# A four-layer graph network on one core: a third sort of the edges, the edge records fetched in the dense stages, and node degrees summed in layer 1

## The reference

```python
edge_index = jnp.stack([src, dst])
xn = _layernorm(x, axis=-1)
x = x + _L0_gnn_ref(xn, ..., src, dst) + _L0_mix_ref(xn[None], ...)[0]
x = x + _L0_ffn_ref(_layernorm(x, axis=-1)[None], ...)[0]
...
# layer 0, edges
e = jax.nn.leaky_relu(el[src] + er[dst], NEG_SLOPE)
score = e @ attn
smax = jax.ops.segment_max(score, dst, num_segments=N)
ex = jnp.exp(score - smax[dst])
ssum = jax.ops.segment_sum(ex, dst, num_segments=N)
out = jax.ops.segment_sum(el[src] * (ex / ssum[dst])[:, None], dst, num_segments=N)
```

## Time and profile before

| what | us |
|---|---|
| median of three runs | 9504.5 (9498.88 to 9510.58) |
| the profiled execution on the device | 9501.75 |
| its span in the profile | 9499.6 |
| sort by target, with keys, chunk order and parts | 262.6 |
| all stages of the order by source | 398.6 |
| opening of layer 0 | 716.1 |
| attention of layer 0 | 1341.0 |
| the nine dense stages from `close0` to `open2` | 1035.7 |
| sum pass of layer 1 | 1113.5 |

### The profile page before, as it was taken

One profiled execution on the slowest core, in us unless ns is written; L12 is line 12 of the kernel. 1 busy time (PEld: TensorE's weight loads), 2 busy tenths in 40 slices (PEclk: granted clock), 3 DMA queues, 4 the chain that ended last, 5 costly groups with the idle time before them and its releaser, 6 DMA issues. The chain is left out here.

```text
span 9499.6 us, 92227 instructions
## 1 busy us (share of the span) xinstructions
PE 6037.2 (64%) x26290; PEld 4579.3 (48%) x26290; DVE 4854.0 (51%) x13537; ACT 2032.6 (21%) x5038; POOL 4347.3 (46%) x4412
## 2 busy tenths in 40 slices
PE   0012306999996875555755555553883788886699
PEld 0001105788874443333544433342872677775466
DVE  7773406888884532222343222275114588887433
ACT  0001003555542210000120000022221233333322
POOL 0476775666650047777004777702001577772000
PEclk9998657999997887777777777775996777777799
DMA  0001003333330133333102333301871233331000
GB/s 14 6 2 36 10 2 94 89 90 90 90 80 9 54 114 105 105 105 105 24 12 75 105 105 105 105 7 24 301 272 41 78 97 99 97 98 45 12 14 21
DMA packets 404417, 697.22 MB, mean 73 GB/s; under 512 B 154143, under 2 KB 267784, under 8 KB 403421
## 3 DMA queue, kind: packets, MB, share of 16 engines
q0 software_dynamic: 206848, 480.68, 18.8%
q1 hardware_dynamic: 197076, 210.68, 7.0%
HBM read 631.46 MB, written 59.47 MB: 73 GB/s over the span
## 5 line engine op out<-in xcount | busy, mean ns | idle before, releaser
L641 PE MATMUL sum_sum<-sum_rows,sum_hot 128*125 128x256 f32 x3520 | 1268.3, 524 | 956.4 <-DMA sum_rows<-el_table,dst_order_row 465.9
L658 POOL DMA_INDIRECT att_rows<-el_table,dst_order_row x1520 | 1476.3, 971 | 755.8 <-issue 377.5
L641 PEld LDWEIGHTS sum_sum<-sum_rows,sum_hot 128*125 128x125 f32 x3520 | 868.5, 258 | 1356.2 <-issue 1029.2
L602 POOL DMA_INDIRECT sum_rows<-rel_table,src_order_row x880 | 836.9, 951 | 888.2 <-ACTq L593 620.4
L602 POOL DMA_INDIRECT sum_rows<-el_table,dst_order_row x880 | 835.3, 949 | 806.0 <-ACTq L593 538.3
L554 POOL DMA_INDIRECT dst_order_record<-records,dst_order_row x784 | 835.1, 1065 | 582.0 <-PEq L458 297.3
L624 DVE TENSOR_TENSOR gnn_acc<-gnn_acc,sum_sum 125x256 f32 x440 | 181.4, 412 | 1591.1 <-PE sum_sum L641 1585.7
L800 PE MATMUL att_found<-gnn_to_dst,att_hot_t 125*128 x1760 | 442.5, 395 | 40.9 <-issue 40.3
L824 PE MATMUL att_sum<-att_rows,att_hot 128*125 128x261 f32 x1760 | 443.7, 394 | 0.0
L1140 PE MATMUL att_sum<-att_rows,att_hot 128*125 128x265 f32 x1280 | 421.2, 485 | 2.5 <-DVE att_rows L1031 2.4
L658 POOL DMA_INDIRECT dst_order_record<-el_table,dst_order_row x240 | 240.9, 1004 | 333.8 <-SPq L962 239.2
(11 more groups left out here) (775 smaller groups left out, 12136.3 us busy)
## 6 DMA issues: line engine op xcount, KB each, us to landing
block_w<-in_L_ffn_W_dram SPq DMA_DIRECT2D x112, 512.0 KB, 6.2
block_w<-in_L_ffn_W_dram SPq DMA_DIRECT2D x56, 1024.0 KB
att_rows<-el_table,dst_order_row POOLq DMA_INDIRECT x1520
rel_table<-open_st SPq DMA_DIRECT2D x25, 784.0 KB
sum_rows<-rel_table,src_order_row POOLq DMA_INDIRECT x880, 2.7
sum_rows<-el_table,dst_order_row POOLq DMA_INDIRECT x880, 2.7
dst_order_record<-records,dst_order_row POOLq DMA_INDIRECT x784, 2.3
pairs<-zeros SPq DMA_DIRECT2D x1, 7168.0 KB
```

Of the source, the lines that this page charges most:

```text
L602: nc.gpsimd.indirect_dma_start(rows[l][:, g, :], None, table, bass.IndirectOffsetOnAxis(ap=o["row"][:, k:k + 1], axis=0)).then_inc(s[f"row ...
L641: last = nc.tensor.matmul(slot(u), hot[u % HOTS_S][:, g, :], rows[l][:, g, :], start=(g == 0), stop=(g == G - 1))
L658: nc.gpsimd.indirect_dma_start(rows[l][:, g, 0:width], None, table, bass.IndirectOffsetOnAxis(ap=o["row"][:, k:k + 1], axis=0)).then_inc(s ...
```

## The change

`order_by_pair` sorts the edges by target and source: the low bits of the key are the source, so `row` is the source at once and nothing has to be fetched for layer 0. `order_by_edge` sorts by target and edge number a third time, after the order by source, and keeps the edge numbers in `edge`; it has no unit tiles. `fetch_records` gathers by `edge`, and no longer in the sorts or in `open0`, but in nine dense stages up to `open2`, after which `unpack_records` stands. Records have three words. `build_attend0` loses the three columns (L860 and L761 go) and the degree phase goes. Layer 1's `build_sums` makes the degrees: it loads target, weight and attribute of all edges, and for 200 of the 220 units VectorE makes one-hot marks of the node in its tile and of the tile, the latter also times weight and attribute, and TensorE multiplies them into one PSUM bank. In that pass there are seven row buffers instead of ten; in both passes 12 marks and 12 PSUM slots, and `BEHIND` is 8.

```diff
-HOTS_S = 14
-SLOTS_S = 16
-BEHIND = 10
+HOTS_S = 12
+SLOTS_S = 12
+BEHIND = 8
+DEGS_S = 2
-REC = 4
+REC = 3
-SHARES = (14, 190, 30, 6, 8, 18, 14)
-EARLY = sum(SHARES)
+SHARES = {"close0": 78, "open0g": 66, "ffn0s": 42, "ffn0e": 100, "open1": 156, "close1": 25, "open1g": 37, "ffn1e": 146, "open2": 134}
...
+def order_by_pair(nc, c, I, o):
...
+                own(v.tensor_scalar(dst_i[:], dst_i[:], 12, 0x20000000, ALU.logical_shift_left, ALU.bitwise_or))
+                own(v.tensor_tensor(edges, dst_i[:], src_i[:], ALU.bitwise_or))
...
+                own(v.tensor_scalar(o["row"][:, main], bits, 0xFFF, None, ALU.bitwise_and))
+        build_unit_tiles(nc, c, "dst_tiles", o)
+def order_by_edge(nc, c, I, o):
...
+                own(nc.vector.tensor_scalar(o["edge"][:, 0:CHUNKS_S], key_c[:].bitcast(I32), 0x1FFFF, None, ALU.bitwise_and))
...
-        nc.gpsimd.indirect_dma_start(o["record"][:, k, :], None, o["records"], bass.IndirectOffsetOnAxis(ap=o["row"][:, k:k + 1], axis=0)
+        nc.gpsimd.indirect_dma_start(o["record"][:, k, :], None, o["records"], bass.IndirectOffsetOnAxis(ap=o["edge"][:, k:k + 1], axis=0)
...
+                def make_ends(n, own):
+                    l, part, here = n % DEGS_S, slice(n * G, n * G + G), slice(n % DEG_UNITS * G, n % DEG_UNITS * G + G)
+                    if n % DEG_UNITS == 0:
+                        part_edges(n, own)
+                    if n >= DEGS_S:
+                        dve.wait_ge(s["degree_summed"], n - DEGS_S + 1)
+                    v.tensor_tensor(end[l][:], row_of(iota_p[:, 0:R], G), col_of(in_tile[:, here], R), ALU.is_equal)
+                    own(v.tensor_tensor(terms[l][:, :, 2, :], row_of(iota_p[:, 0:TILES], G), col_of(of_tile[:, here], TILES), ALU.is_equal))
+                    v.tensor_tensor(terms[l][:, :, 0, :], terms[l][:, :, 2, :], col_of(of_edge["weight"][:, part], TILES), ALU.mult)
+                    v.tensor_tensor(terms[l][:, :, 1, :], terms[l][:, :, 2, :], col_of(of_edge["attr"][:, part], TILES), ALU.mult).then_inc(s["ends_ready"], 1)
...
+                    if u < N_D:
+                        pe.wait_ge(s["ends_ready"], u + 1)
+                        for g in range(G):
+                            last = nc.tensor.matmul(deg_p[:, 0:3 * TILES], end[u % DEGS_S][:, g, :], terms[u % DEGS_S][:, g, :, :].rearrange("p k t -> p (k t)"),
+                                                    start=(u == 0 and g == 0), stop=(u == N_D - 1 and g == G - 1), skip_group_check=True)
+                        last.then_inc(s["degree_summed"], 1)
...
-                    v.scalar_tensor_tensor(to[:, 0:D + 1], to[:, 0:D + 1], corr[u % 2][:], sums[u % 2][:, 0:D + 1], ALU.mult, ALU.add)
-                    v.tensor_tensor(to[:, D + 1:], to[:, D + 1:], sums[u % 2][:, W:S], ALU.add).then_inc(s["added"], 1)
+                    v.scalar_tensor_tensor(to, to, corr[u % 2][:], sums[u % 2][:, 0:S], ALU.mult, ALU.add).then_inc(s["added"], 1)
...
-                    a.copy(own_rows[:, :, W:S], o["record"][:, u * G:u * G + G, 1:4])
...
-    order_by_dst(nc, c, I, by_dst)
-    order_by_src(nc, c, I, by_src, [record_share(nc, by_dst, n) for n in range(6)])
+    order_by_pair(nc, c, I, by_dst)
+    order_by_src(nc, c, I, by_src)
+    order_by_edge(nc, c, I, by_dst)
```

More of the change, by code:

```diff
@@ L513, in order_by_dst @@
+def order_by_edge(nc, c, I, o):
+    with ExitStack() as ctx:
+        sb = lambda n, sh, d=F32: ctx.enter_context(nc.sbuf_tensor(f"edge_order_{n}", sh, d))
+        T, turned = [sb(f"keys{k}", [P, ROWS_A]) for k in range(2)], ctx.enter_context(nc.psum_tensor("edge_order_turned", [P, ROWS_A], F32))
         dst_i, edge_i = (sb(n, [R, CHUNKS], I32) for n in ("dst_i", "edge_i"))
         edges = T[0][0:R, 0:CHUNKS].bitcast(I32)
-        with phase(nc, "dst_keys", "loaded", "placed", "chain") as s, nc.Block() as block:
+        with phase(nc, "edge_keys", "loaded", "placed", "chain") as s, nc.Block() as block:
@@ L582, in batches_of, with build_sums @@
     return u // BATCH + 1
-def build_sums(nc, c, tag, table, o, w, acc):
+def build_sums(nc, c, tag, table, o, w, acc, degrees=None):
     assert UNITS_S % BATCH == 0 and HOTS_S >= BEHIND + BATCH and SLOTS_S >= BEHIND + BATCH and BATCH % 2 == 0
+    lanes = LANES_D if degrees else LANES_S
     with ExitStack() as ctx:
-        rows = [ctx.enter_context(nc.sbuf_tensor(f"{tag}_rows{l}", [P, G, D], F32)) for l in range(LANES_S)]
+        rows = [ctx.enter_context(nc.sbuf_tensor(f"{tag}_rows{l}", [P, G, D], F32)) for l in range(lanes)]
         hot = [ctx.enter_context(nc.sbuf_tensor(f"{tag}_hot{l}", [P, G, R], F32)) for l in range(HOTS_S)]
@@ L1619, in kv, with open1 @@
         return last
-    build_open(nc, c, 0, m["X"], m["XN"], m["XNT"], loads, units, post, stores, kv, keep_blocks(c, 1.0 / NODES, m["KV"]), hand=(ACT.Sqrt,), pool_work=pool_work, st_lanes=1, pair=True)
-def open1(nc, c, m, I, dram):
+    build_open(nc, c, 0, m["X"], m["XN"], m["XNT"], loads, units, post, stores, kv, keep_blocks(c, 1.0 / NODES, m["KV"]), hand=(ACT.Sqrt,), st_lanes=1, pair=True)
+def open1(nc, c, m, I, dram, pool_work):
     def loads(sb):
@@ L1692, in kv @@
         return last
-    build_open(nc, c, 2, m["X"], m["XN"], m["XNT"], loads, units, post, stores, kv, keep_blocks(c, 1.0, m["KV"], ones=True), hand=(ACT.Exp,))
+    build_open(nc, c, 2, m["X"], m["XN"], m["XNT"], loads, units, post, stores, kv, keep_blocks(c, 1.0, m["KV"], ones=True), hand=(ACT.Exp,), pool_work=pool_work)
 def open3(nc, c, m, I, dram):
@@ L3261, in own_loops @@
             own(leaky(v, top[:]))
-            own(v.tensor_copy(attr[:], by_dst["record"][:, :, 2]))
+            own(v.tensor_copy(attr, by_dst["record"][:, :, 2]))
         bulk(nc, "loops3", own_loops)
```

198 lines of the change are left out of this document (125 added, 73 removed).

## The result

The changed kernel takes 9457.2 us (median of five runs, 9453.7 to 9461.5) against 9504.5 before: a ratio of 0.995 with a 95% interval from 0.9935 to 0.9964, 47 us. The forecast was 9474, a gain of 30. The profiled execution's span fell by 44.1 us, from 9499.6 to 9455.5; what follows is a cut of that at the barriers.

A forecast was written before the change was run, and what follows sets the result against it. No engine bounds the whole kernel: barriers close each phase, which lasts as long as its slowest engine. Terms from +262.6 (third sort) and +72 (dense stages) to -337.4 (layer 0's opening) sum to -30 us: 9474 us from 9504.5, range 9405 to 9535.

The forecast's parts named there:

- The third order: A third sort of the edges, by target and edge number, alone in its stage and hidden by no engine: +262.6 us.
- the 2.5 us: First order, now by target and source: a second load and 24 more four-element copies, estimated at +2.5 us.
- The dense stages: 784 gathers placed in nine dense stages, overrunning them through GpSimd's list, holds by VectorE and drains: +72 us together.
- rival 1: Gathers in the nine dense stages do not wait for VectorE: +15 instead of +72 us, 9417 us; chance 0.15.
- VectorE itself pays nothing: In the nine dense stages, gathers cost VectorE no time: busy 212.9 us in the sort without them, 213.3 with.
- Operations that read PSUM: In the dense stages, VectorE operations reading PSUM hold no gathers; otherwise the sum would grow by some 20 us.
- Rival 3: Gathers in the nine dense stages cost 1.58 us each, overrunning them by 245 us: 9647 us; chance 0.08.
- the 1.33 set against it: The forecast's own cost per gather in us, compared with about 1.38, where the overrun of 102 us decides against the change.
- The sum pass: Layer 1's sum pass stays paced by GpSimd while making the degrees: +6 us, bounds 0 and +74.
- rival 4: Layer 1's sum pass becomes TensorE's, 200 units losing 0.37 us each, 74 us: 9542 us; chance 0.10.
- The attention: Layer 0's attention loses two operations per unit, but VectorE waits for TensorE's lookup: 0, bounds 0 and -33 us.
- rival 2: Layer 0's attention follows VectorE, so dropping 220 adds of 151 ns gains 33 us: 9441 us; chance 0.11.

The follow-up runs named there:

- experiment 3: The changed kernel with VectorE's second and third operation per turn in layer 0's expert stage made one-input SBUF copies: that stage took 143.8 us against 152.1.

## Why the prediction was right, and where it was not

- **What bounds the kernel.** Right: stage by stage, the engine that ended the stage decided. The opening lost 338.6 us with GpSimd's queue, the sort by source exactly its 13.0, and 457 us more of VectorE's work showed only where VectorE ended a stage: in the third sort.
- **The third order.** +262.6 against +261.4. The first order cost more than the 2.5 us: its keys 3.0, and the unit tiles, whose 24 copies are 48 now, another 2.9.
- **The dense stages.** The mechanism is right: the hold is as the timeline of before gave it, and rival 1 falls with it. Six of the nine ended with GpSimd, at 111.9, 60.9, 152.1, 217.4, 40.8 and 178.1 us, all but the last within 1.5 us of what was worked out. For layer 0's experts that is luck, since two sizes in the sum were off and cancelled: a pair of operations held 0.61 + 0.28 = 0.89 us, not 1.15, since the requests do not fall anywhere in the 1.25 us, as the average assumed; and the drain (from the last gather's end to the stage's end) was 9.1 us there, not 5. In layer 2's opening, 4.6 us under the forecast, both were smaller than assumed: the gathers were held 6.4 us in all (132.85 - 134 x 0.944), not 8.7, and the drain was 4.1, not 6. Layer 1's experts ended with VectorE, at 198.5 us, and not with GpSimd's list at 200.6: its holds were 7.8 us, not 11.5.
- **"VectorE itself pays nothing"** was not quite right; only the sort that it was read from shows no loss. In the gate openings of layers 0 and 1, L1381 took up to 0.60 and 0.64 us where before none of its operations took over 0.42, VectorE was busy 0.9 and 0.6 us longer, and the stages were 1.3 and 0.7 us longer.
- **Operations that read PSUM** were counted as free, without a row for it: right, 59 of 59.
- **Rival 3** (1.58 us per gather) falls: with their holds the nine stages took 1.24 to 1.48, from the first gather to the last. The mean that the forecast itself implied was about 1.35 (784 gathers at 1.249 and 78 us of holds), not the 1.33 set against it.
- **The sum pass and rival 4.** The terms were right in kind: the pass stayed GpSimd's. The two short operations with both inputs in SBUF were put at 6 us; the gathers lost 2.4 under them, and 3.3 with all that the degrees bring. Rival 4 falls: TensorE was busy 782.5 us of 1116, at a mean granted clock of 0.81, higher than the 0.75 without the degrees, and still waited 309 us for rows.
- **The attention** was put at 0 with bounds 0 and -33; -6.2 came, so rival 2 falls. By the prediction's own sign ("if the attention drops below 1335 us") it was wrong here, at 1334.8. The step that failed is that the wait for TensorE would take up the whole add: about 2 us of it came through (1.1 in the middle 120 of 220 units), out of a bound that should have been 15 and not 33. The larger part was in no term; the order of the rows is some of it, the rest is open.
- The gain came out 17 us larger than the forecast, 14 of them in the spans: 4 in the dense stages, 3 in the sum pass, 6 in the attention and 4 in stages that scatter, less 3 in the other terms together. The other 3 are the 2.75 us by which the kernel before ran below its median when it was profiled.

## What to carry to other kernels

When idle time of one engine is filled with work from another stage, what counts is the list's own end, its holds and its drain against the stage's length. Cost the list stage by stage and leave several per cent of slack: at 784 gathers in nine stages the overrun was 68 us, at 559 it was 3. The emptiest stage is often the one from which the work was just taken; the opening that had been the bottleneck at 504 gathers hides 238 for 4 us. Which operations of VectorE hold GpSimd's gathers depends on where their operands lie: one input in PSUM freed the gathers at the same length of the operation (mean 0.944 us after 1.121), though keeping PSUM longer cost more here than it gave. A stage of one profile can come out as expected for another reason: look at the granted clock in its last units before a few us are given to a cause.

## What the runs showed of the hardware that was not expected

- A gather is also held by a one-input copy from SBUF to SBUF that runs at nearly twice the pace of the others (1280 elements in 0.83 us); a copy of 2560 in 2.82 us did not hold one. Such a copy took 1.06 us instead of 0.83 where a gather had begun 0.53 us ahead of it.
- One-input operations with two scalars per row from SBUF held some gathers a little: 45 of the 179 that met the marks of L655 in layer 1's sum pass took over 1.0 us (up to 1.06).
- The release is exact: 0.817 us from the end of VectorE's two-input operation to the end of the gather, with a spread of 0.002 over 133 gathers. Behind the first of two fast copies it was 0.98.
- Gathers and VectorE's operations fall into step, so that averages over an even spread were too high in two places: 65 meetings where 108 were worked out, 0.89 us per pair where 1.15 was.
- From the end of the last gather to the end of a stage that GpSimd ended took 3.0 to 9.1 us, and not by the number of gathers: 4.1 behind 134, 4.9 behind 156, but 7.1 behind 78 and 9.1 behind 100, the last with fewer holds too (experiment 3). Why is open.
- Layer 0's attention ran a little faster when the rows of a target were gathered in ascending order, with the same instructions: 713.0 to 713.3 us for 120 units in seven profiles, 714.0 in one with another order.
